# A new step order for a hand-pipelined decoder layer, with its first loads reordered

## The reference, cut to what matters

```
x = x + proj(causal_linear_attention(ln(x)))          # 16 heads of 16, phi = elu + 1     (stage a)
q = ln(x);  qp, kp = prob(q), prob(ctx)               # tanh*0.499+0.5, divided by its row sum
sid  = (qp - kp) @ (log qp - log kp).T                                                    # (stage b)
f    = (ctx - softmax(-sid/16) @ ctx) @ W_diff.T + b_diff + q
x = x + ln(f + gelu(ln(f) @ W1.T + b1) @ W2.T + b2)   # hidden 1024, exact gelu
h    = ln(x);  idx = top_128(h @ w_router)            # 128 of 256 tokens                 (stage c)
s    = h[idx];  s = s + attention(rms(s)*g1)          # 16 heads, causal in rank order, softmax
s    = s + (silu(u @ W1.T) * (u @ W2.T)) @ W3.T       # u = rms(s)*g2, width 682
x    = x + h with the rows idx replaced by s
```

## Time and profile before

| | |
|---|---|
| device time, three runs | 886.56, 887.78, 888.12 us; median 887.78 |
| span of the profiled execution | 886.5 us, 21236 instructions |
| what lies around the span | about 1.3 us (median less span) |
| mean granted clock of TensorE | 0.987 |
| one round of the loop | 49.67 us (439.86 to 489.53 us) |

### The profile page before, as it was taken

How to read it: one execution, slowest core, us unless ns; L and a number is a source line. 1 busy time by engine, 2 the same in 40 slices (tenths; PEclk the granted TensorE clock), 3 DMA queues, 4 the chain that set the end, 5 groups by cost and what they waited for, 6 DMA issues and landing times.

```text
span 886.5 us, 21236 instructions
## 1 busy us (share of the span) xinstructions
PE 810.7 (91%) x7219; PEld 699.5 (79%) x7219; DVE 724.2 (82%) x1689; ACT 560.2 (63%) x1518; POOL 276.6 (31%) x443
## 2 busy tenths in 40 slices
PE   7778799999999999999999999999999999988875
PEld 4567678888888888888898888888898888867644
DVE  4777789898988989898998989898998989784642
ACT  3463548577676758577666758577667758575541
POOL 0021514234251524234251514333251514233211
PEclk8899999999999999999999999999999999999999
DMA  8310111202020110102020111202020111101010
GB/s 295 101 42 25 48 50 37 61 19 84 18 83 6 47 53 36 59 18 83 18 83 6 55 45 36 65 12 83 18 83 6 59 41 36 55 2 49 8 54 7
DMA packets 31223, 44.02 MB, mean 50 GB/s; under 512 B 2512, under 2 KB 23120, under 8 KB 31184
## 3 DMA queue, kind: packets, MB, share of 16 engines
q1 hardware_dynamic: 27696, 32.93, 10.9%
q0 software_dynamic: 2048, 6.30, 2.4%
q10 hardware_dynamic: 1440, 4.28, 1.5%
HBM read 28.81 MB, written 14.70 MB: 49 GB/s over the span
## 4 chain that ended last, share of the span: by engine, by line
PE 56%; DVE 16%; ACT 15%; issue 8%; DMA 2%; POOL 2%; SPq 1%; DVEq 0%; ACTq 0%; POOLq 0%
PE bank L1131 14%; ACT w_raw_or_stage_c L721 9%; PE bank L1235 4%; PE bank L1253 4%; PE bank L1315 3%; PE bank L1509 3%; PE bank L1390 3%; PE bank L1323 3%; PE bank L1139 3%; PE bank L1293 3%; PE bank L1147 3%; ACT L721 2%; PE bank L1415 2%; DVE prob L915 2%; PE bank L1435 2%
## 5 line engine op out<-in xcount | busy, mean ns | idle before, releaser
L676 ACT ACTIVATE prob<-bank,b_folded 128x256 f32<-128x256 f32 x128 | 53.7, 471 | 99.9 <-PE bank L1131 99.7
L870 DVE TENSOR_TENSOR a_s<-bank,const 128x512 f32<-128x512 f32 x112 | 72.6, 685 | 47.5 <-PE bank L1235 25.8
L721 ACT ACTIVATE w_raw_or_stage_c<-bank,c_nmax 128x128 f32<-128x128 f32 x256 | 90.2, 403 | 3.2 <-DVE c_nmax L1044 3.0
L538 POOL DMA_INDIRECT out<-w_raw_or_stage_c,row_of_slot_out x16 | 17.3, 1081 | 182.1 <-DVE w_raw_or_stage_c L1098 182.1
L721 ACT ACTIVATION_READ_ACCUMULATOR w_raw_or_stage_c<-bank,c_nmax 128x1 f32 x256 | 62.0, 242 | 0.0
L787 DVE TENSOR_TENSOR b_s_lo<-prob,b_s_hi 128x512 fp32r<-128x512 f32 x64 | 43.2, 675 | 21.0 <-ACT b_s_hi L563 21.0
L1426 PE MATMUL bank<-const,w_raw_or_stage_c 128*128 128x128 f32 x256 | 40.3, 280 | 16.6 <-ACT w_raw_or_stage_c L721 16.6
L860 DVE RECIPROCAL a_e<-a_e 128x512 f32<-128x512 f32 x16 | 53.5, 3342 | 0.0
L1426 PEld LDWEIGHTS bank<-const,w_raw_or_stage_c 128*128 128x128 f32 x256 | 28.0, 140 | 26.1 <-ACT w_raw_or_stage_c L721 16.9
L1131 PE MATMUL bank<-b_s_hi,w_mlp_hi 128*128 128x256 f32 x256 | 45.1, 298 | 2.5 <-ACT prob L676 1.4
L1044 DVE TENSOR_REDUCE c_nmax<-bank 128x4 f32<-128x512 f32 x64 | 41.7, 677 | 6.4 <-PE bank L1415 6.4
(11 more groups left out here) (256 smaller groups left out, 2698.7 us busy)
## 6 DMA issues: line engine op xcount, KB each, us to landing
token_rows<-norm_x_rms SPq DMA_DIRECT2D x16, 513.0 KB, 3.9
x_in<-in_x SPq DMA_DIRECT2D x16, 256.0 KB, 3.4
x<-in_x SPq DMA_DIRECT2D x16, 256.0 KB, 2.8
qc<-in_ctx SPq DMA_DIRECT2D x16, 256.0 KB, 2.7
b_f<-in_ctx_t SPq DMA_DIRECT2D x16, 256.0 KB, 2.9
out<-w_raw_or_stage_c SPq DMA_DIRECT2D x16, 256.0 KB, 2.2
w_raw_or_stage_c<-in_w ACTq DMA_DIRECT2D x4, 512.0 KB, 5.8
...
```

Source lines behind the costliest of these rows:

```text
L676: act_in(prob[:, 2 * (j % 2) + n, :], b0[:, n * T:(n + 1) * T], ACT.Gelu, bias=b1p[:, f:f + 1]).then_inc(b_gelu.sem, 1)
L721: act_in(c_e[g % 2][:, j * R:(j + 1) * R], C_SCORES[g][:, j * R:(j + 1) * R], ACT.Exp, bias=c_nmax[:, n:n + 1], accum_out=c_den[:, head:he ...
L870: tt(heads(A_MASKED[t][n][:, :]), heads(A_SCORES[n][:, :]), tri.unsqueeze(1).broadcast_to([P, 4, P]), ALU.mult).then_inc(a_scput.sem, 1)
```

## The change

All of `ORDER` is written anew, starting at another point of the round; each step keeps the row that it works on relative to the others, with "+" set accordingly. What changes on an engine is the order of neighbouring steps:

- PE: `a_q` ahead of `c_xo`, `a_k` ahead of `c_h2tp`, `c_sbc` ahead of `c_gu_0`, `b_up_2` ahead of `b_down_0`, `b_up_3` ahead of `c_score`, `c_etp_1` ahead of `b_down_3`.
- ACT: `b_vput` ahead of `b_tanhq`; `a_qout` and `a_kout` ahead of `c_h2sq` and `c_h2hi`; `b_gelu_0` ahead of `c_qkput`; `b_dput` and `b_rput` ahead of `c_tanh_1`; `b_gelu_2` ahead of `b_ghi_1`.
- DVE: `a_tlo` ahead of `b_onormed` and `b_done`; `b_pnorm` ahead of `c_h2put`; `a_mean` behind `b_glo_1`; `c_y` and `b_glo_0` earlier; `b_vq` behind `c_sel`; `c_etput_2` ahead of `c_dinv`.
- POOL: `b_qb` and then `c_rms1` between `c_rstd` and `c_h2rms`; `b_kept` behind `b_frstd`; `c_put` and `b_fb2` behind `a_rstd`; `c_hx` ahead of `c_obs`.

The semaphore `vec_in` becomes three (`rows_in`, `cols_in`, `w_qk_in`), and the waits of the weight splits, the bias fold and `b_mean` need only `cols_in`. SP issues the column vectors right behind the first three raw loads, and the bulky first loads behind the next row of x and the third weight split. The six scalings of stage c's weights on POOL move from `c_rstd(0)` to `a_rstd(0)`. ACT loads its exp table at the start, and the first `a_qout` does not. `WEIGHTS_AT` and `WARM_AT` are new; the filler matmuls go from 69 to 157.

```
 ORDER = """
-c_w2 b_frstd+ c_gthi_0++ c_gtlo_0++ c_ob+ b_fput+ b_fmean+ c_gthi_1++ a_kput+ a_sput+ b_fd+ c_gtlo_1++ c_hsc+
-a_mask+ c_ff_0++ a_state+ b_fnormed+ a_den+ c_w6 a_dput+ c_ff_1++ a_scput_0+ a_scput_1+ b_hlo+ a_scput_2+
-a_scput_3+ c_w8 c_ht+ a_score_0+ c_hput+ b_htp+ a_mean b_hhi+ a_scput_4+ c_qkput+ c_qk+ b_up_0+ c_w4
-a_score_1+ a_scput_5+ a_scput_6+ b_gelu_0+ c_v+ a_att_0+ b_up_1+ a_scput_7+ a_att_1+ b_down_0+ c_w1 c_vput+
-b_ghi_0+ b_glo_0+ b_up_2+ c_score+ b_gelu_1+ c_y++ b_up_3+ c_put++ b_ghi_1+ a_dinv+ c_w7 b_glo_1+ b_gelu_2+
-a_y+ a_rstd b_glo_2+ a_proj+ c_max_0+ c_w3 b_rstd c_max_1+ b_ghi_2+ b_qb a_yhi+ b_gelu_3+ b_down_1+ b_orstd+
-b_down_2+ a_ylo+ c_max_2+ a_normed c_w0 c_etp_0+ b_down_3+ c_exp_0+ c_rstd a_done+ c_h2rms+ b_mean c_etp_1+
-b_ghi_3+ c_exp_1+ c_max_3+ c_w9 c_etp_2+ c_exp_2+ a_tp c_exp_3+ c_etp_3+ b_v c_dtp+ c_rms1 b_glo_3+ c_etput_0+
-c_att+ b_normed b_o+ b_tanhk c_xo+ c_etput_1+ a_thi c_dbc+ b_omean+ a_q c_dinv+ c_dput+ c_etput_2+ c_h2tp+ a_k
-c_w5 c_keep+ c_etput_3+ c_gu_0+ c_sbc a_val b_tanhq b_onormed+ b_done+ c_obs c_h2sq+ c_hx+ c_pick b_vput c_o+
-c_mean a_tlo c_idx c_h2put+ c_h2hi+ b_pnorm c_gu_1+ c_h2lo+ a_qout b_log c_normed b_diff c_rscore b_vq b_dtp
-c_tanh_0+ c_rank a_kout c_sel c_tanh_1+ b_rtp b_ratio b_kept c_idxput b_dput c_gu_2+ b_sid b_fb2 a_phi_q
-b_rput c_gate_0+ a_phi_k c_gtp_0+ a_vput c_gate_1+ a_csum c_gtp_1+ a_kq a_ktp b_sexp
+b_down_3++ c_etp_2++ b_qb+ c_rms1+ b_o++ c_h2rms++ c_exp_1++ a_tp+ c_etput_2++ c_dinv++ b_omean++ c_etp_3++
+c_etput_3++ b_v+ c_dtp++ c_keep++ a_tlo+ c_hx++ b_ghi_3++ c_obs+ c_exp_2++ c_exp_3++ c_att++ b_tanhk+ a_thi+
+b_onormed++ c_w5 c_dbc++ b_done++ c_o++ c_pick+ a_q+ c_mean+ b_pnorm+ c_h2put++ c_xo++ c_normed+ a_k+ c_h2tp++
+c_rscore+ a_val+ c_sbc+ b_diff+ c_gu_0++ c_idx+ c_h2lo++ c_dput++ b_vput+ c_gu_1++ b_dtp+ b_tanhq+ a_qout+
+a_kout+ c_rank+ c_h2sq++ b_frstd+ c_sel+ b_vq+ b_rtp+ c_idxput+ c_gu_2++ b_sid+ b_ratio+ c_h2hi++ c_gtp_0++
+c_gtp_1++ b_log+ c_tanh_0++ b_dput+ a_ktp+ c_gate_0++ b_rput+ b_fd+ a_phi_q+ c_tanh_1++ a_state+ a_phi_k+
+c_gate_1++ a_csum+ c_ff_0++ a_vput+ a_kq+ c_gtlo_0++ b_fput+ b_fmean+ b_sexp+ c_gtlo_1++ a_kput+ c_gthi_0++
+a_sput+ a_den+ c_w2 c_ff_1++ c_ht+ a_score_0+ b_kept+ a_mask+ c_hsc+ b_htp+ c_gthi_1++ b_fnormed+ a_dput+ c_qk+
+c_hput+ c_y++ a_scput_0+ b_up_0+ a_scput_1+ b_hlo+ c_ob+ b_hhi+ a_score_1+ c_v+ a_scput_2+ a_scput_3+ a_att_0+
+b_gelu_0+ a_rstd b_ghi_0+ a_scput_4+ b_up_1+ b_fb2+ a_att_1+ b_glo_0+ c_qkput+ a_scput_5+ b_gelu_1+ a_scput_6+
+a_scput_7+ c_vput+ a_dinv+ b_up_2+ a_y+ c_put++ b_gelu_2+ b_ghi_1+ b_down_0+ a_yhi+ b_rstd b_up_3+ b_glo_1+
+b_ghi_2+ a_mean c_score+ a_ylo+ a_proj+ b_glo_2+ b_down_1+ a_normed c_max_0+ b_gelu_3+ c_max_1+ c_max_2+
+b_down_2+ c_etp_0+ a_done+ b_mean c_max_3+ c_etp_1+ b_orstd+ c_rstd b_glo_3+ c_etput_0+ c_etput_1+ c_exp_0+
+b_normed
 """.split()
...
-WEIGHTS_AT = {(0, "c_w0"): 2, (0, "a_qout"): 1, (0, "c_w1"): 1, (1, "c_w2"): 1, (1, "c_w3"): 1, (1, "c_w4"): 2, (1, "c_w5"): 1, (1, "c_w6"): 1, (1, "c_w7"): 1, (1, "c_w8"): 1, (1, "c_w9"): 1}
+WEIGHTS_AT = {(0, 'b_orstd'): 1, (1, 'b_omean'): 1, (1, 'c_w5'): 1, (1, 'c_y'): 1, (1, 'a_rstd'): 2, (1, 'b_normed'): 1, (2, 'c_idx'): 1, (2, 'a_csum'): 1, (2, 'c_w2'): 1, (2, 'b_gelu_0'): 2, (2, 'c_rstd'): 1}
...
             for n in range(NRAW):
-                if n == DC:
-                    sp.dma_start(const[:, EARLY:NCONST], consts[:, EARLY:NCONST]).then_inc(const_rest.sem, 16)
                 sp.dma_start(raw[:, n, 0:loads[n][1]], loads[n][0]).then_inc(raw_in[n].sem, 16)
-            sp.dma_start(x1[:, :, :], x_rows[0]).then_inc(a_kept.sem, 16)
-            sp.dma_start(qc[:, TT:2 * TT, :], ctx_rows[0]).then_inc(ctx_in_s.sem, 16)
-            sp.dma_start(b_f1[:, :, :], ctx_t_rows[0]).then_inc(ctx_t_in.sem, 16)
-            sp.dma_start(bc[:, :, :], vec_bc).then_inc(vec_in.sem, 16)
-            sp.dma_start(cols[:, :], vec_cols).then_inc(vec_in.sem, 16)
-            sp.dma_start(wcqk[:, :, :], w_cqk).then_inc(vec_in.sem, 16)
-            sp.dma_start(wcv[:, :, :], w_cv).then_inc(w_plain.sem, 16)
-            sp.dma_start(wo[:, :, :], w_out).then_inc(w_plain.sem, 16)
-            sp.dma_start(wd[:, :, :], w_diff).then_inc(wd_in.sem, 16)
+            sp.dma_start(cols[:, :], vec_cols).then_inc(cols_in.sem, 16)
+            sp.dma_start(const[:, EARLY:NCONST], consts[:, EARLY:NCONST]).then_inc(const_rest.sem, 16)
...
             next_x(0)
+            sp.wait_ge(raw_hi.sem, NRAW)
+            sp.dma_start(qc[:, TT:2 * TT, :], ctx_rows[0]).then_inc(ctx_in_s.sem, 16)
+            sp.dma_start(b_f1[:, :, :], ctx_t_rows[0]).then_inc(ctx_t_in.sem, 16)
+            sp.dma_start(x1[:, :, :], x_rows[0]).then_inc(a_kept.sem, 16)
+            sp.dma_start(wd[:, :, :], w_diff).then_inc(wd_in.sem, 16)
+            sp.dma_start(bc[:, :, :], vec_bc).then_inc(rows_in.sem, 16)
+            sp.dma_start(wcqk[:, :, :], w_cqk).then_inc(w_qk_in.sem, 16)
+            sp.dma_start(wcv[:, :, :], w_cv).then_inc(w_plain.sem, 16)
+            sp.dma_start(wo[:, :, :], w_out).then_inc(w_plain.sem, 16)
             keep_x(1)
...
             def a_rstd_(b):
                 power(b, a_mean, a_mv[:, :, 1], LN_EPS, a_rs[:, :], a_rstd)
...
                 if first(b):
-                    pool.wait_ge(vec_in.sem, 48)
+                    pool.wait_ge(cols_in.sem, 16)
+                    pool.wait_ge(w_qk_in.sem, 16)
                     pool.wait_ge(w_plain.sem, 32)
...
                     if loads[n][3:]:
-                        act_e.wait_ge(vec_in.sem, 48)
+                        act_e.wait_ge(cols_in.sem, 16)
...
             def a_qout_(b):
-                nc.scalar.preload_act_table_set("natural_log_exp_and_others")
+                if not first(b):
+                    nc.scalar.preload_act_table_set("natural_log_exp_and_others")
                 act_e.wait_ge(*a_qk(b, 1))
...
+            nc.scalar.preload_act_table_set("natural_log_exp_and_others")
             act_e.wait_ge(ones_set.sem, 1)
```

More of the change, by code:

```diff
@@ L63 @@
 FIRST = STEPS[0][0]
-WEIGHTS_AT = {(0, "c_w0"): 2, (0, "a_qout"): 1, (0, "c_w1"): 1, (1, "c_w2"): 1, (1, "c_w3"): 1, (1, "c_w4"): 2, (1, "c_w5"): 1, (1, "c_w6"): 1, (1, "c_w7"): 1, (1, "c_w8"): 1, (1, "c_w9"): 1}
-WARM_AT = {(0, 'a_q'): 2, (0, 'a_ktp'): 3, (1, 'a_state'): 3, (1, 'a_score_0'): 1, (1, 'a_score_1'): 5, (1, 'a_att_0'): 3, (1, 'a_proj'): 9, (1, 'b_rtp'): 2, (1, 'b_sid'): 1, (2, 'a_score_0'): 1, (2, 'b_htp'): 1, (2, 'b_up_0'): 2, (2, 'a_att_0'): 1, (2, 'b_up_3'): 1, (2, 'c_sbc'): 3, (2, 'b_sid'): 1, (3, 'c_ht'): 2, (16, 'c_etp_3'): 1, (16, 'c_gu_0'): 1, (16, 'c_idx'): 3, (17, 'b_htp'): 1, (17, 'b_up_1'): 2, (17, 'c_etp_0'): 1, (17, 'c_etp_2'): 1, (17, 'c_etp_3'): 1, (17, 'c_xo'): 1, (17, 'c_idx'): 2, (18, 'c_ht'): 6, (18, 'c_score'): 1, (18, 'c_etp_0'): 4, (18, 'c_etp_1'): 1, (18, 'c_etp_2'): 1, (18, 'c_etp_3'): 1}
+WEIGHTS_AT = {(0, 'b_orstd'): 1, (1, 'b_omean'): 1, (1, 'c_w5'): 1, (1, 'c_y'): 1, (1, 'a_rstd'): 2, (1, 'b_normed'): 1, (2, 'c_idx'): 1, (2, 'a_csum'): 1, (2, 'c_w2'): 1, (2, 'b_gelu_0'): 2, (2, 'c_rstd'): 1}
+WARM_AT = {(1, 'a_tp'): 6, (1, 'a_q'): 5, (1, 'a_ktp'): 1, (1, 'a_state'): 2, (1, 'a_den'): 2, (1, 'a_score_0'): 3, (1, 'a_score_1'): 1, (1, 'a_att_0'): 5, (1, 'a_proj'): 9, (2, 'a_tp'): 2, (2, 'b_rtp'): 4, (2, 'b_sid'): 3, (2, 'b_fd'): 2, (2, 'a_score_0'): 4, (2, 'b_htp'): 2, (2, 'b_up_0'): 5, (2, 'a_att_0'): 3, (3, 'b_v'): 1, (3, 'c_sbc'): 5, (3, 'c_idx'): 6, (3, 'b_dtp'): 2, (3, 'b_sid'): 3, (3, 'b_fd'): 2, (3, 'c_ht'): 5, (17, 'c_etp_3'): 2, (17, 'c_xo'): 1, (17, 'c_h2tp'): 9, (17, 'c_sbc'): 4, (17, 'b_htp'): 2, (17, 'b_up_2'): 3, (17, 'c_etp_1'): 1, (18, 'c_etp_3'): 2, (18, 'c_dtp'): 1, (18, 'c_att'): 2, (18, 'c_xo'): 4, (18, 'c_h2tp'): 2, (18, 'c_sbc'): 7, (18, 'c_gu_2'): 2, (18, 'c_gtp_1'): 1, (18, 'c_ht'): 3, (18, 'c_qk'): 1, (18, 'c_score'): 2, (18, 'c_etp_0'): 8, (18, 'c_etp_1'): 3, (19, 'c_etp_2'): 3, (19, 'c_etp_3'): 3, (19, 'c_dtp'): 1, (19, 'c_xo'): 1, (19, 'c_h2tp'): 2, (19, 'c_gu_0'): 2, (19, 'c_gu_2'): 1, (19, 'c_gtp_1'): 1}
 WARM_START = 14
@@ L269, in decoder @@
         FOLD = {LOADS_A + k: k for k in range(DC)}
-        const_in, const_rest, vec_in, w_plain, w_scaled = sig("const_in"), sig("const_rest"), sig("vec_in"), sig("w_plain"), sig("w_scaled")
+        const_in, const_rest, rows_in, cols_in = sig("const_in"), sig("const_rest"), sig("rows_in"), sig("cols_in")
+        w_qk_in, w_plain, w_scaled = sig("w_qk_in"), sig("w_plain"), sig("w_scaled")
         raw_in = [sig(f"raw_in{n}") for n in range(NRAW)]
@@ L451, in a_rstd_ @@
                 power(b, a_mean, a_mv[:, :, 1], LN_EPS, a_rs[:, :], a_rstd)
+                if first(b):
+                    pool.wait_ge(cols_in.sem, 16)
+                    pool.wait_ge(w_qk_in.sem, 16)
+                    pool.wait_ge(w_plain.sem, 32)
+                    for k in range(DC):
+                        for w, factor in ((wcqk[:, k, 0:D], 1.0 / HD ** 0.5), (wcqk[:, k, D:2 * D], 1.0), (wcv[:, k, :], 1.0)):
```

(8 more changed lines are left out.)

## The result

The changed kernel takes 896.58 us in the median of four runs (896.20 to 898.05), the kernel before 887.86 (886.56 to 888.12): a ratio of 1.0106, 95% interval 1.0092 to 1.0119. It is slower by about 9 us, where 866 had been forecast. The profiled execution has a span of 894.4 us, 7.9 more than the 886.5 before.

The account below looks back on a forecast made before the run. PE was taken to bound the loop rounds (48.05 of 49.67 us busy), a chain of waits the start. Terms -13 - 1 - 2 - 2 - 4 = -22 gave a span of 864.5, with 1.3 around it 866 us; range 852 to 880.

Parts of the forecast that it names:

- The start: Row 0 up to a_y: third weight split no longer waits for stage c's weights; -13 us, bounds -16 and -6.
- The rest of the first rows: After row 0's start: weight splits further apart, -1 us; the 2.5 us wait for a_tlo goes, -2 us.
- The tail: Last row: c_rms1 no longer behind c_h2rms, b_up_3 ahead of c_score, c_etput_2 ahead of c_dinv; -4 us.
- The rounds of the loop: 13 steady rounds: a period of 49.5 us against 49.67, -2 us in all.
- the three pieces of the period: A loop round: c_gu_2 to a_att_0 17.06 us, on to c_mean 23.0, back to c_gu_2 over POOL 9.4.
- The one on the other side: Loop: POOL's chain ahead of the gate becomes the bound, period 51.7 us, time 893; chance 0.12.
- PE alone bounds the rounds: Loop: with POOL's way short, PE sets a round of 48.6 us, time 854; chance 0.17.
- POOL waits for DVE in every round: Loop: c_rms1 takes 3.17 us and b_qb 1.92, period 50.6, time 880; chance 0.05.
- Nothing comes of it: Whole kernel: what the start wins is lost in the rounds, time 887 us; chance 0.03.
- At nothing: Added fillers (up to +3 us), moved scalings, later bulky loads, new semaphores and another round boundary priced at no cost.

Follow-up runs that it names:

- the run with three moves: The changed kernel with three POOL steps moved: b_fb2 behind b_kept, b_qb ahead of b_orstd, c_hx behind c_obs; 872.3 us, ratio 0.983.
- the last version: The changed kernel with b_fb2 behind b_kept and b_qb ahead of b_orstd on POOL, a_mean ahead of b_glo_1 on DVE; 857.5 us, ratio 0.966.

## Why the prediction was wrong, step by step

*The start*, forecast -13, measured -10.1 at `a_dinv` and -10.7 at the end of `a_y` (35.17, not 32.8): right in kind, the size off by 2 to 3. `a_q` began at 9.28 and took 1.68, as walked. What I had not in the walk is 2.25 us of fillers on the way, five of them at 25.24 in the chain, 0.45 each, and a wait for the low part of the third load ahead of the first `a_scput` (20.62). The fillers are no net loss there: without any, `a_dinv` begins at 31.7, later and not earlier.

```profile
9.28 1.68 PE bank L1135 x12
...
25.24 2.25 PE bank L1521 x5
```

*The rest of the first rows*, -3 forecast: the first two intervals between one `a_dinv` and the next came out 0.2 shorter in all. The 2.5 us wait for `a_tr_lo` is indeed gone from PE's waits of 88 to 142 us, but it bought nothing. In these intervals three tensor_scalar instructions of DVE, one `a_normed` and one `b_pnorm` among them, took 1.3 to 1.4 instead of 0.4; that just these took the gain is not shown.

*The tail*, -4 forecast, -5.0 measured. The last `c_rms1` starts at 851.09, right behind `c_rstd`, and in the run that puts it back behind `c_h2rms` the store of its rows begins 2.4 later, near the 2.1 that I had for it.

*The rounds of the loop*, -2 forecast, +23.0 between the first and the last `a_dinv` (the -0.2 of the first two intervals is in it): this is the step that failed. I priced the three pieces of the period with DVE's instructions at the times that they had before, and looked at POOL and DVE side by side only to ask how long POOL waits for DVE. `b_qb` and `c_rms1` were given long times because DVE is busy beside them; that `b_qb` would make `b_pnorm` longer, and `b_fb2` `a_normed`, was not asked, though for row 0 I had counted POOL's adds beside `b_pnorm`. In the event POOL's steps ran at their short or middle times (`b_qb` 1.32, the four of `c_rms1` 2.4), and DVE paid. PE's piece from `c_gu_2` to the end of `a_att_0` came out as priced, at 17.1. From the end of `a_att_0` to the end of `c_mean` I had 23.0; it took 24.6: 0.99 more is `a_normed`, and 0.61 is a wait for `a_rstd` ahead of it, a new one that I had not counted. (The waits that I let close did close.) From `c_mean` to `c_gu_2` I had 9.4 over POOL and the gate; it took 10.0, and not on that path: as in the kernel before, it went over DVE (`b_pnorm`, then `c_sel`), a way that I had not priced. What these two took beyond their former times is 1.40 of the 10.0. With the two adds moved away the round is 49.3 and the time 866.5: what failed was this one interaction, worth 30 us. That 866.5 is so near the forecast is in part luck. In that run the start gives 10.5 instead of 13, the first two intervals nothing instead of 3, the rounds 5.8 instead of 2 and the tail 5.9 instead of 4; the errors cancel.

The rule of the Trainium skill that I weighed (page "SBUF — State Buffer", section "SBUF: two separate sides") holds for both engines: of a GpSimd instruction and a DVE instruction "in a 2-port perf mode, or with two SBUF inputs" it says that whichever "starts first gets the pair for the whole instruction; the other fully blocks". The runs agree: with an add of 1.28 or 0.73 the first tensor_scalar beside it ends 0.04 to 0.16 us behind the add, and the subtraction with two SBUF inputs is held too. I had read it as a price for POOL alone. The runs also show that not every DVE instruction is held. In the changed kernel `b_kept` lies beside DVE instructions that read one input out of a PSUM bank, and they keep their 0.68 (the two in the first row overlap by 0.08):

```profile
467.34 1.29 POOL L440 TENSOR_TENSOR norm_x_rms<-x,vectors_by_row 128x512 f32<-128x512 f32 x1 [2.08 <-ACT w_raw_or_stage_c L697]
```

```profile
466.95 1.29 DVE L874 TENSOR_TENSOR a_s<-bank,const 128x512 f32<-128x512 f32 x2 [0.59 <-PE bank L1239]
468.15 0.68 DVE L791 TENSOR_TENSOR b_s_lo<-bank,b_s_hi 128x512 fp32r<-128x512 f32 x1
```

In the run with three moves, `b_qb` lies beside a copy out of a PSUM bank and beside statistics, and both keep their 0.68 and 0.69:

```profile
429.42 1.27 POOL L440 TENSOR_TENSOR q_bias<-qc,vectors_by_row 128x512 f32<-128x512 f32 x1 [2.63 <-DVE b_f L968]
```

```profile
429.19 0.68 DVE L1055 COPY c_et<-bank 128x512 f32<-128x512 f32 x1
...
429.95 0.69 DVE L796 BATCH_NORM_STATS2 f_st<-b_f 128x6 f32<-128x256 f32 x2
```

*The rivals.* The one on the other side gave 893 and a period of 51.7, close to what came, but by another mechanism: POOL's chain at its longest times, ahead of the gate. `c_h2rms` brought forward by itself gave only what `c_sel` gave, so its price was right by chance. *PE alone bounds the rounds*: the last version comes to the 48.6 that I had named for it, with PE busy for 98% of a round; but its chain of waits lies on PE for only about half of the round (430.4 to 453.8), so that PE alone bounds it is not shown. *POOL waits for DVE in every round* did not come: `b_qb` took 1.32 and `c_rms1` 2.4, not 1.92 and 3.17. *Nothing comes of it* had the right shape, but the rounds lost more than start and tail had won (23.0 against 15.1). *At nothing*: true of the loop, the semaphores and the scalings as far as any run shows; not of the fillers, without which the changed kernel is 12.9 us slower.
